# Four of the opening's twelve bf16 filling products become float32 products on tiles of TensorE's array

## The reference

```python
# layer 0
xn = _ln_last(x, ln1_g, ln1_b)                       # norm over the last axis
q, k, v = [_conv(_conv(xn, w1, 0), w3, 1) for w1, w3 in qkv]
score = jnp.einsum('bhpd,bhpe->bhde', k, q) / scale
attn = jnp.einsum('bhpd,bhde->bhpe', v, softmax(score))
x = _conv(attn, o_w, 0) + x
xn = _ln_last(x, ln2_g, ln2_b)
gate = gelu(_conv(_conv(xn, g1, 0), g3, 1))
info = _conv(_conv(xn, i1, 0), i3, 1)
x = _conv(gate * info, r1, 0) + x
# layer 1
out = leaky_relu(instance_norm(conv2d(x, conv1_w, conv1_b)))
x = x + refine(out)          # a 3x3 conv, a sigmoid mask, attention over 3x3 neighbours
```

## Time and profile before

| what | value |
|---|---|
| median of 2 runs | 212.07 us (212.03 to 212.11) |
| span of the profiled execution, first to last instruction | 210.1 us |
| that execution's own time, beside its span | not recorded apart; against the median, 2.0 us lie around the span |
| PE busy | 184.5 us, 88% |
| DVE busy | 161.3 us, 77% |
| ACT busy | 119.4 us, 57% |
| POOL busy | 70.5 us, 34% |
| mean granted PE clock | 0.989 |

### The profile page before, as it was taken

One profiled execution on the slowest core, in us unless ns is written; L12 is line 12 of the kernel. 1 busy time (PEld: TensorE's weight loads), 2 busy tenths in 40 slices (PEclk: granted clock), 3 DMA queues, 4 the chain that ended last, 5 costly groups with the idle time before them and its releaser, 6 DMA issues.

```text
span 210.1 us, 5374 instructions
## 1 busy us (share of the span) xinstructions
PE 184.5 (88%) x2158; PEld 104.0 (50%) x2167; DVE 161.3 (77%) x382; ACT 119.4 (57%) x251; POOL 70.5 (34%) x62
## 2 busy tenths in 40 slices
PE   1799879879986999899997999899799998899972
PEld 1349339333353756643576455743423345565741
DVE  6798799988768859599497986994928576992682
ACT  2175273655259461967692862775845583966850
POOL 7600803150310403660007613750044003670290
PEclk9999999978999999999999999999999999999998
DMA  6412031001501000001000040001001000000002
GB/s 199 80 57 58 2 100 50 3 0 37 163 0 50 3 5 10 3 3 39 0 3 0 3 147 13 6 3 46 4 6 47 3 0 10 8 5 8 5 2 103
DMA packets 10154, 6.75 MB, mean 32 GB/s; under 512 B 7248, under 2 KB 8496, under 8 KB 10128
## 3 DMA queue, kind: packets, MB, share of 16 engines
q1 hardware_dynamic: 9888, 5.82, 10.2%
q10 hardware_dynamic: 240, 0.58, 0.7%
HBM read 3.30 MB, written 1.05 MB: 21 GB/s over the span
## 4 chain that ended last, share of the span: by engine, by line
PE 53%; DVE 22%; ACT 12%; issue 5%; DMA 3%; POOL 1%; SPq 1%; DVEq 0%; ACTq 0%
PE ps L1455 20%; PE ps L1375 5%; PE ps L1368 5%; PE ps L1402 5%; PE ps L1498 4%; ACT xw L703 3%; ACT p_t L720 3%; DVE sh_in L316 3%; PE ps L1533 3%; DMA w3b<-in_w_gi 2%; ACT sh_x L608 2%; PE ps L1544 2%; DVE ln_out L968 2%; PE ps L1522 2%; PE ps L1587 2%
## 5 line engine op out<-in xcount | busy, mean ns | idle before, releaser
L1455 PE MATMUL ps<-sh_ln,w_gi 96*64 96x512 f32 x192 | 44.6, 615 | 1.7 <-DVE sh_ln L316 1.7
L473 POOL TENSOR_TENSOR ln_s<-ln_s,neg_half 128x16 f32<-128x16 f32 x7 | 20.4, 2909 | 55.5 <-DVE ln_s L947 55.5
L608 ACT ACTIVATE sh_ln<-ln_out 32x512 f32<-32x512 f32 (+2 forms) x46 | 25.6, 557 | 14.6 <-DVE ln_out L968 5.5
L1455 PEld LDWEIGHTS ps<-sh_ln,w_gi 96*64 96x64 f32 x192 | 15.4, 140 | 25.9 <-issue 25.8
L1402 PE MATMUL ps<-w_qk,sh_ln 128*128 128x128 f32 x192 | 23.2, 278 | 0.4 <-issue 0.4
L1402 PEld LDWEIGHTS ps<-w_qk,sh_ln 128*128 128x128 f32 x192 | 22.2, 192 | 1.9 <-DMA sh_ln<-ln_out 0.9
L1498 PE MATMUL ps<-sh_in,w_in 96*32 96x256 f32 x384 | 22.8, 380 | 0.0
L1368 PE MATMUL ps<-busy 128*128 128x512 bf16 x68 | 19.4, 419 | 1.3 <-issue 1.2
L608 ACT ACTIVATE sh_x<-x 32x496 f32<-32x496 f32 (+1 forms) x20 | 12.3, 616 | 9.2 <-DVE x L1093 9.0
L1498 PEld LDWEIGHTS ps<-sh_in,w_in 96*32 96x32 f32 x384 | 11.9, 109 | 10.3 <-issue 3.0
L498 POOL TENSOR_TENSOR omm<-ones,msk 128x512 f32<-128x512 f32 x4 | 7.1, 1780 | 22.6 <-DVE msk L1169 22.6
(11 more groups left out here) (142 smaller groups left out, 334.6 us busy)
## 6 DMA issues: line engine op xcount, KB each, us to landing
sh_ln<-ln_out SPq DMA_DIRECT2D x27, 64.0 KB, 2.1
x_res<-in_x SPq DMA_DIRECT2D x4, 256.0 KB, 2.8
out_x<-out_s SPq DMA_DIRECT2D x4, 256.0 KB, 2.0
x_norm<-in_x SPq DMA_DIRECT2D x3, 256.0 KB, 2.9
kc<-in_shape_consts ACTq DMA_DIRECT2D x1, 450.0 KB, 4.9
w3b<-in_w_gi SPq DMA_DIRECT2D x1, 288.0 KB, 5.0
x_norm<-in_x SPq DMA_DIRECT2D x2, 128.0 KB, 2.8
xm<-xm SPq DMA_DIRECT2D x8, 25.5 KB, 1.9
```

Source lines behind the costliest of these rows:

```text
L473: nc.gpsimd.tensor_tensor(ln_s[n][:, 3, :], ln_s[n][:, 2, :], neg_half[:, :], ALU.pow)\
L608: return nc.scalar.activation(o, i, ACT.Copy)
L1455: mm = nc.tensor.matmul(ps[EC * h:EC * h + EC, GI_BANKS[n], :], w_gi[:, dy, n % 2, :], xs[:, n // 2, y:y + H // 2, 0:W], start=(dy == 0), ...
```

## The change

Before, twelve bf16 filling products on the whole array stand ahead of PE's wait for image 0. After, there are eight of them. Then PE waits for `s_zero` to reach 2 (`ones` is set) and runs float32 filling products on tiles: three rounds of eight products with a 32 x 64 weight and 256 columns (eight tiles), three rounds of sixteen with a 32 x 32 weight and 128 columns (sixteen tiles), and one round of four with a 32 x 128 weight and 512 columns (four tiles). The four row blocks write PSUM banks 1, 3, 4 and 5. The five bf16 products behind the wait stay. (EC is 64, BLK 256, C 32, P 128 and R 4.)

```diff
+            def stay_busy_on_tiles(rounds, width, columns):
+
+                banks = (1, 3, 4, 5)
+                for _ in range(rounds):
+                    for r in range(R):
+                        rows = slice(C * r, C * r + C)
+                        for at in range(0, P, width):
+                            nc.tensor.matmul(ps[at:at + width, banks[r], 0:columns], ones[rows, 0:width],
+                                             ones[rows, 0:columns], start=True, stop=True)
+
             pe.wait_ge(s_busy, 1)
-            stay_busy(12, 5)
+            stay_busy(8, 5)
+            pe.wait_ge(s_zero, 2)
+            stay_busy_on_tiles(3, EC, BLK)
+            stay_busy_on_tiles(3, C, P)
+            stay_busy_on_tiles(1, P, 2 * BLK)
             pe.wait_ge(g_im[0].sem, g_im[0].done(0))
             stay_busy(5, 5)
             pe.wait_ge(s_wready, W_QKV)
```

## The result

The change makes the kernel slower: 217.03 us (216.85 and 217.22) against 212.07, a ratio of 1.0273 with an interval of 1.0198 to 1.0348. More executions, run later as one of the experiments, gave 215.88 us (six, 215.11 to 218.06) against 212.13 (29, 209.78 to 214.34), a ratio of 1.0189 (1.0146 to 1.0233). The kernel before spreads far more than its first two executions showed: 67 later ones lie between 208.84 and 214.51 us.

A forecast was written before the change was run, and what follows sets the result against it. It took the opening's chain of waits, with the filling products before `qk(0, 0)` as links, as the bound: 212.07 + 2.94 for the longer filling - 1.77 for a clock fall going away = 213.2 us, range 211.4 to 217.2.

The forecast's parts named there:

- The cost of the tile parts and the delay of the opening: First filling: tile parts take 1.32, 1.28 and 0.88 us at the high clock; the opening ends 2.0 to 2.9 us later.
- The sum: Opening: removed and added filling, shape changes and five bf16 products added up; products end at 18.35 us instead of 15.41.
- rival C: Opening: at most four tiles work together, eight- and sixteen-tile parts 2.64 us each; 217.7 or 215.9 us; chance 0.17.
- D: Opening: tile products don't count for the clock, which rises late; 216.3 to 219.8 us; chance 0.08.
- What is late next: nothing: From `qk(0, 0)` to `gate_info(0, 0)`: nothing takes up the delay, so the whole opening moves by 2.0 to 2.9 us.
- The other direction: Opening: a filling shorter than now would bring `qk(0, 0)` forward by up to 1.8 us.
- What may come back: `gate_info`: the clock's fall at 45.02 us, after PE's longest rest, may go away; 0 to -1.77 us.
- A: Tiles overlap, opening 2.0 to 2.9 us later, the clock's fall in `gate_info` goes away; 213.2 us; chance 0.38.
- B: Same overlap and later opening, but the clock's fall in `gate_info` stays; 214.1 to 215.0 us; chance 0.26.
- The added instructions: First filling: 76 calls, 152 entries and as many loads, counted by their run time in the opening.
- about 25 ns: Sixteen-tile part: the skill's floor between product starts would make 96 entries 2.4 us; the sum used 13.3 ns, 1.28 us.

The follow-up runs named there:

- e2: Kernel before, opening untouched, the eight bf16 fillers ahead of `attn_out(0)` replaced by 78 small float32 tile products (296 PE instructions more): 212.39 us, ratio 1.0010.
- e10: Changed kernel with 55 small tile products ahead of `attn_out(0)` to realign its program, and nine instead of two bf16 fillers before `gate_info`: 213.69 us, ratio 1.0132.
- e4: Kernel before with nine instead of two bf16 filling products in the rest ahead of `gate_info`: 210.17 us, ratio 0.9974.
- e3: Changed kernel with five bf16 filling products in each of two rests, ahead of `conv1(0)` and between it and the average: 216.92 us, ratio 1.0265.
- e1: Kernel before with 21 instead of 12 bf16 products in the first filling, 18 PE instructions more: 212.21 us, ratio 1.0044.
- e5: Changed kernel with 58 small tile products replacing the eight bf16 ones ahead of `attn_out(0)`, PE's program 512 instructions longer than before: 213.15 us, ratio 1.0055.
- e6: Kernel before, opening untouched, with 83 small float32 tile products replacing the eight bf16 ones ahead of `attn_out(0)`, 316 PE instructions more: 213.42 us, ratio 1.0056.
- e9: Changed kernel with all 76 tile products cut to 32 columns, the same instructions: 211.66 us, ratio 1.0080.
- e8: Kernel before, rests before `gate_info` and around `conv1(0)` filled using full-array float32 products, other fillers exchanged to keep program length: 210.89 us, ratio 0.9956.

## Why the prediction was wrong

I forecast 213.2 us and no difference that can be told; it came out 5.0 us slower on the first two executions and 3.8 on the medians of more. By its own steps:

- *The cost of the tile parts and the delay of the opening* were right, if a little low. The sum had `qk(0, 0)` at 18.35 us; the second profile has 18.69 with a filling that began 0.5 us late. The executions differ in when the filling begins (8.85 to 9.95 us) and in how soon behind that the clock rises, so only profiles with a like rise compare. With a rise 2.4 to 2.6 us behind it, the time from the start of the filling to `qk(0, 0)` is 8.16 us in the first profile of the change and 4.83 in e2; with one at 4.1 to 4.4, 8.98 in e10 and 5.68 in e4. It costs 3.1 to 3.3 us, and I had 2.9. (In the sum, 12.65 us is the fourth load from the end of the slow ones, not the fifth; the ninth product starts there within 0.1 us all the same.) More than four tiles do work together (the parts took 1.48 and 1.42 us, not 2.64 each), so rival C is out. D is out as well: five bf16 products behind the tile part run at the high pace in every profile, and in the second profile the clock rose while tile products ran.
- *What is late next: nothing* held. Both profiles carry the delay of `qk(0, 0)` unaltered to `gate_info` and beyond. The other direction, that a shorter filling would bring everything forward by up to 1.8 us, doesn't hold: in e2 `qk(0, 0)` started 1.30 us sooner and `gate_info` 0.21, because `qk(0, 1)` then waited 0.89 us for the planes of image 1.
- *What may come back* failed, and with it the choice of A over B. I took the fall of the clock to hang on one long rest, because shorter ones "brought no fall" in the one profile that I had the earlier trace rows. After the change the fall stayed in both profiles, at 45.9 and 48.2 us, and no execution of the change has a mean clock above 0.992 (15 of the 67 of the kernel before have 0.995 or more). In the first profile the clock also fell at 69.8, right behind the two rests of 1.19 and 1.26 us that I had called harmless. That fall isn't the change's own: e2, with the opening of before, has it at 66.25, behind the same two rests, and the second profile of the change hasn't. e3, with the rests filled, fits that they make it, but its one profile doesn't show it. That filling the long rest keeps the clock up is shown by e4; that the rest alone brings the fall isn't, since e1 and e5 mostly keep the clock with it open. So the term stood at -1.77 us and was 0 in one profile and +1.6 in the other.
- *The added instructions* had no term beyond their own run time. They cost 1.5 us in the first profile and 0.75 in the second, 120 us and more behind the change. e6 makes such waits without touching the opening, and e5 takes most of them away by adding still more instructions. The places say the same. In the stretch behind pair 3, PE stops behind the first entry of L1498 in all four profiles with 297 more instructions (the change twice, e2, e9), ten entries earlier with 317 (e3, e6), eleven later with 18 (e1) and twenty later with 513 (e5, whose wait is counted too). In pieces of 256, 317 is 20 more than 297, 18 is 23 less and 513 is 40 less, and an entry with its load is two instructions: the place moves as the count says. How long PE stops there is open: the same program has 1.03 us in one profile and 0.34 in the other.

With B in place of A (+2.9) and 0.75 to 1.5 us for the program, the sum would have been 215.8 to 216.5 us. What is left open is why some kernels (e1, e5) keep the clock in most executions where others with as long a rest before `gate_info` don't.

## What to carry to other kernels

A filling product is also instructions: prefer the form that holds the engine longest per instruction (a gain of that alone isn't shown here: e8 against e4), and after any edit that changes an engine's instruction count look for stops without a releaser in its densest stretches, far behind the edit. A fall of the clock in one profile is a sample, not a property of the place; take several executions before a term is built on one, and fill the rest instead of hoping that a shift avoids it. And filling that ends where real work could start is on the path, so what replaces it must not be longer at either clock.

## What the runs showed of the hardware that I had not expected

PE seems to run out of its own program at times. In the trace of the changed kernel one 16 KB transfer of queue q8 runs from 198.32 to 199.28 us, beside the run of L1561 (the first row has 8 KB of queue q14 as well), and then comes the stop, with no transfer in flight:

```profile
198.00:199.50 1.50, 1.50 (x68) 1.07 (x67) 1.32 (x3) 1.48 (x8) 0.00 (x0) 1.00 0.06 16
199.65:200.65 1.00, 0.00 (x0) 0.00 (x0) 0.96 (x2) 0.95 (x3) 0.00 (x0) 1.00 0.00 0
```

The stops, 0.3 to 1.0 us, come in or right behind the small tile products of L1561, of which 64 take 1.05 us. That the stop is a late piece of program is inferred, not read from a row: its place moves with the count of instructions in pieces of 256, as told above, and each of the eight marked stops behind 135 us, in six profiles, ends 1.2 to 1.6 us after a 16 KB transfer of q8 has ended. The Trainium skill, "Runtime: NRT & Kernel Launch", section "Instruction fetch mechanics", says that instructions come in blocks of 16 KB or 256 instructions, which agrees with 18 transfers and 0.29 MB for PE's 4630 entries and loads here, and that the cost of crossing a block is mostly hidden. Here most crossings show no stop either, but with 297 or 317 instructions more, two or three of them, in these dense stretches, cost 0.75 to 2.5 us together.

Products on tiles start closely behind each other. Sixteen tiles with 128 columns took 1.42 us for 96 entries, 14.8 ns each; with 64 columns 156 entries span 1.83 us in e2, of which one lasts 0.21, so (1.83 - 0.21) / 155 = 10.5 ns:

```profile
25.51 1.83 PE L1629 MATMUL ps<-ones 32*32 32x64 f32 x156
```

The 14.8 ns is twice the 6.9 ns that sixteen tiles in full overlap would need, so these runs don't show that all sixteen work at once. Both spacings are below the about 25 ns that the prediction weighed, which by the Trainium skill, "TensorE: Matmul & The Clock Gate", section "Wait — 56ns, not 53.3ns?", is the closest that products start behind each other.

The clock's rise and falls aren't fixed to the program: the same filling got to its high pace at 14.33 us in the kernel before and at about 11.7 in e2, whose opening is the same to the instruction:

```profile
11.39 0.15 PEld L1368 LDWEIGHTS ps<-busy 128*128 128x128 bf16 x1 [0.28 <-issue]
11.73 2.04 PEld L1368 LDWEIGHTS ps<-busy 128*128 128x128 bf16 x10 [0.18 <-issue]
```
